# Four graph layers in one pipeline: layer 0 turned by DMA, hi and lo halves in one transfer, two biases moved to GpSimd

## The chip, the cores and the metric

The kernel runs on one core of a Trainium2 chip. The metric is the device time of one execution in microseconds; lower is better. Engines: TensorE (PE in the profile; PEld is its weight load), VectorE (DVE), ScalarE (ACT), GpSimd (POOL), and SyncE (SP), which here only issues DMAs.

## The reference

Input x has 128 graphs of 128 nodes with 256 features, and all graphs share one adjacency matrix. Four layers follow each other, each as x = x + layer(relu(layernorm(x))):

```
L0  h = X W;  e = leaky_relu(att_self + att_neigh^T), masked by adj;  out = [softmax(e) h | h]      W: 256x128
L1  out = deg * (x Wi + b) + adj (x Wj)                                                            W: 256x256 each
L2  8 heads of 32: q, k, v = h W^T + b;  softmax(q k^T / sqrt(32), masked) v;  then Wo, bo
L3  as L0 with one head of 256: softmax(leaky_relu(e_src + e_dst), masked) Wh
```

## The kernel before, in words

The work is cut into 64 groups of two graphs (`GROUP = 2`). A group's activations x stay in SBUF (`x`, 128 partitions x 2 x 256, fp32, 11 buffers), and every other tile of a group is double. All the work of a group is a list of some 110 pieces, such as `stats0_0` or `make_query`, whose last digit before the underscore is the layer.

**Software pipeline.** Each engine has one `slot(at)` function, a list written out by hand: `at(3, make_query)` means that in slot t the engine does this piece for group t - 3. `run(slot)` goes through 64 + 7 slots. So each engine's queue is a fixed order that repeats once a slot, and groups of up to eight ages are in it at a time. An engine's instructions run in the order of its queue; a wait on a semaphore (`wait_ge`) holds back all that stands behind it. A slot number says nothing of time between engines: one engine's slot t can run beside another's slot t + 1.

**Numbers.** Products with big weights are done as fp16 triples (`triple`, lines 402 to 407): each factor is split in a high and a low fp16 half, and hi·hi, hi·lo and lo·hi are added up in PSUM. Weights are scaled by 256 first and unscaled when PSUM is read. To split an activation, ScalarE writes the high half with a ReLU or copy (`rows_hi2`, `keep_out`, `rows_hi3`), and VectorE writes the rest (`rows_lo2`, `split_out`, `rows_lo3`).

**Turns.** A product needs its left operand with features on the partitions. For layers 2 and 3, the mixed heads (`out`) and the attention probabilities, SyncE issues transposing DMAs, one for the high and one for the low half (lines 344 to 374; of 512 columns, the probabilities of 2048). Layer 0 is different: it is fp32, its normalized rows are turned by four TensorE transposes (`turn`, line 400), ScalarE copies them out of PSUM (`relu_hi0`), and `feat0` (line 466) is an fp32 matmul, which the profile records as two instructions.

**Layer norm.** VectorE takes bn_stats and bn_aggr; GpSimd adds eps (`add_eps`), negates the mean (`negate_mean`), takes the power -1/2 (`power`) and normalizes the two graphs (`norm_0`, `norm_1`). GpSimd also adds layer 0's second half to x (`add_feat0`) and makes the low halves of the probabilities (`split_head_0` to `_3`).

**Biases.** Those of layer 1 (degree times b1) and of the output projection are added in PSUM by one matmul of 512 columns each (lines 506 and 607).

**SyncE's order**, which holds every DMA of the loop: move_lo3, move_hi3, load_x, move_out_hi, move_out_lo, move_hi2, move_lo2, store_x, move_heads_hi, move_heads_lo. PSUM has eight banks of 512 fp32 columns, and each piece has a fixed one; where two pieces share a bank, an explicit wait keeps them apart.

Of the kernel before, what the change touches and what calls it, by code (L numbers as in the profile page):

```python
# [5 lines left out]
F32 = mybir.dt.float32  # L6
F16 = mybir.dt.float16
# [33 lines left out]
def build(nc, x_in, adj, adj_t, w0, w0_t, a0, w_i, w_j, b1, w_q, w_k, b_qk, w_v, b_v, w_o, b_o, w3, w3_t, a3, out):  # L41
# [7 lines left out]
    with ctx:  # L49
# [18 lines left out]
        w0_f = sb("w0_f", [P, KC, F0W], F32)  # L68
        w_f = sb("w_f", [P, KC, COLS], F32)
# [9 lines left out]
        bo_row = sb("bo_row", [P, D], F32)  # L79
        out_bias = sb("out_bias", [P, D], F32)  # L80

        unit_rows = sb("unit_rows", [P, KC * GROUP * P], F16)
        deg_rows = sb("deg_rows", [P, P], F16)
        b1_rows = sb("b1_rows", [P, D], F16)
        out_rows = sb("out_rows", [P, D], F16)
        qk_bias = sb("qk_bias", [P, 2 * KC * P], F16)
        qk_bias_f = sb("qk_bias_f", [P, 2 * KC * P], F32)
        ones_h = sb("ones_h", [P, P], F16)
# [5 lines left out]
        nmean0, vareps0, rstd0 = (pair(n, [P, GROUP], F32) for n in ("nmean0", "vareps0", "rstd0"))  # L94
# [3 lines left out]
        nmean1, vareps1, rstd1 = (pair(n, [P, GROUP], F32) for n in ("nmean1", "vareps1", "rstd1"))  # L98
# [3 lines left out]
        nmean2, vareps2, rstd2 = (pair(n, [P, GROUP], F32) for n in ("nmean2", "vareps2", "rstd2"))  # L102
# [3 lines left out]
        nmean3, vareps3, rstd3 = (pair(n, [P, GROUP], F32) for n in ("nmean3", "vareps3", "rstd3"))  # L106
        xn3 = pair("xn3", [P, GROUP, D], F32)

        h0t = pair("h0t", [P, KC * GROUP * P], F32)
# [14 lines left out]
        h2_rows_hi = pair("h2_rows_hi", [P, GROUP, D], F16)  # L124
        h2_rows_lo = pair("h2_rows_lo", [P, GROUP, D], F16)
        h2_hi = pair("h2_hi", [P, GROUP * KC, P], F16)
        h2_lo = pair("h2_lo", [P, GROUP * KC, P], F16)
# [1181 lines left out]
```

## Time and profile before

| | |
|---|---|
| median of 3 runs | 1322.18 us (1316.64 to 1323.46) |
| profiled execution | 1312.74 us |
| its span, first to last instruction | 1310.9 us |
| mean granted TensorE clock | 0.972 |
| busy: TensorE, VectorE, ScalarE, GpSimd | 88%, 80%, 76%, 71% of the span |
| DMA queue of the loop | 61.6% of 16 engines |

Busy time is the union of an engine's instructions. Instructions of one engine overlap in its pipeline, so the distance from one start to the next tells what an instruction costs, and its duration tells when its result is there. In the chain of waits "SPq" is SyncE's queue issuing a DMA, and "issue" is time for which the profile shows no reason.

### The profile page before, as it was taken

What the parts mean: (1) busy time and instruction counts of PE and PEld (TensorE: products, weight loads), DVE (VectorE), ACT (ScalarE), POOL (GpSimd) and SP (SyncE); (2) the same over time, 40 slices, a digit from 0 to 9 for tenths busy, and PEclk for the clock granted to TensorE, in tenths of its full rate; (3) what the DMA queues carried; (4) which work ended last, traced back from release to release, by engine and by line L of the source; (5) the groups of instructions that cost most, each with busy time, mean ns of one, the idle gap of its engine ahead of it and who ended that gap; (6) DMA issues with size and microseconds to landing.
All of it is one profiled execution on the core that took longest, in us unless ns stands there. A gap on an engine that the chain in (4) does not pass through costs nothing.

```text
span 1310.9 us, 39708 instructions
## 1 busy us (share of the span) xinstructions
PE 1158.1 (88%) x15385; PEld 967.8 (74%) x15385; DVE 1052.9 (80%) x2913; ACT 1001.4 (76%) x2824; POOL 936.7 (71%) x1606
## 2 busy tenths in 40 slices
PE   3578999999998999999999999998999998999855
PEld 3467878777877877787777877777878787777743
DVE  3468888888887988898888888888888888888752
ACT  2367888888878878887887888778888887888752
POOL 1357777877776777777778777877787777778540
PEclk7699999999999999999999999999999999999996
DMA  5025766665776666677656766666677556776652
GB/s 178 9 50 106 122 106 123 130 132 117 129 132 115 123 130 131 123 126 131 134 116 128 133 124 124 130 130 121 124 130 138 122 123 128 127 123 122 126 111 51
DMA packets 514492, 156.56 MB, mean 119 GB/s; under 512 B 478208, under 2 KB 514304, under 8 KB 514304
## 3 DMA queue, kind: packets, MB, share of 16 engines
q1 hardware_dynamic: 514304, 154.03, 61.6%
q8 instruction: 122, 2.00, 0.6%
q14 instruction: 66, 0.54, 0.2%
HBM read 19.73 MB, written 16.78 MB: 28 GB/s over the span
## 4 chain that ended last, share of the span: by engine, by line
PE 25%; ACT 19%; DVE 17%; DMA 16%; SPq 16%; POOL 5%; issue 3%; POOLq 0%; DVEq 0%
DMA h_lo<-h_rows_lo 9%; PE ps L405 5%; PE ps L407 5%; PE ps L406 5%; SPq L362 5%; DMA h_hi<-h_rows_hi 5%; SPq L346 5%; SPq L366 4%; ACT head_prob L1066 4%; ACT head_prob L1058 4%; ACT head_prob L1074 4%; DVE h_rows_lo L912 3%; DVE key_lo L850 2%; DVE head_nmax L865 2%; ACT out_rows_hi L1089 2%
## 5 line engine op out<-in xcount | busy, mean ns | idle before, releaser
L405 PE MATMUL ps<-w_hi,h_hi 128*128 128x256 f16 (+1 forms) x512 | 142.3, 278 | 35.2 <-DMA h_hi<-h_rows_hi 34.9
L406 PE MATMUL ps<-w_lo,h_hi 128*128 128x256 f16 (+1 forms) x512 | 141.6, 277 | 0.0
L407 PE MATMUL ps<-w_hi,h_lo 128*128 128x256 f16 (+1 forms) x512 | 141.5, 276 | 0.0
L406 PE MATMUL ps<-h_lo,w_hi 128*128 128x256 f16 x512 | 140.5, 274 | 0.0
L407 PE MATMUL ps<-h_hi,w_lo 128*128 128x256 f16 x512 | 140.5, 274 | 0.0
L405 PE MATMUL ps<-h_hi,w_hi 128*128 128x256 f16 x512 | 140.5, 274 | 0.0
L405 PE MATMUL ps<-w_hi,agg_hi 128*128 128x256 f16 x512 | 139.8, 273 | 0.0
L406 PE MATMUL ps<-w_lo,agg_hi 128*128 128x256 f16 x512 | 139.3, 272 | 0.0
L407 PE MATMUL ps<-w_hi,agg_lo 128*128 128x256 f16 x512 | 139.1, 272 | 0.0
L1223 POOL TENSOR_TENSOR head_lo<-head_prob,head_hi 128x512 f16<-128x512 f32 x64 | 74.1, 1157 | 85.1 <-ACT head_hi L1085 85.1
L1183 POOL TENSOR_TENSOR x<-x,g 128x256 f32<-128x256 f32 x64 | 44.5, 695 | 110.0 <-ACT g L992 110.0
L1085 ACT ACTIVATE head_hi<-head_prob 128x2048 f16<-128x2048 f32 x64 | 122.7, 1918 | 0.0
L854 DVE SCALAR_TENSOR_TENSOR v_lo<-ps,v_hi 128x512 f16<-128x512 f32 x64 | 44.4, 694 | 81.3 <-ACT v_hi L1053 81.3
L405 PEld LDWEIGHTS ps<-w_hi,h_hi 128*128 128x128 f16 x512 | 50.2, 98 | 62.5 <-DMA h_hi<-h_rows_hi 54.6
L405 PE MATMUL ps<-v_hi,head_t_hi 128*128 128x33 f16 x1024 | 84.0, 178 | 1.8 <-DMA head_t_lo<-head_lo 1.7
L407 PE MATMUL ps<-v_hi,head_t_lo 128*128 128x33 f16 x1024 | 84.0, 177 | 0.0
L406 PE MATMUL ps<-v_lo,head_t_hi 128*128 128x33 f16 x1024 | 84.0, 177 | 0.0
L1045 ACT ACTIVATE query_hi<-ps 128x512 f16<-128x512 f32 x64 | 38.2, 597 | 58.9 <-PE ps L407 58.9
L405 PEld LDWEIGHTS ps<-v_hi,head_t_hi 128*128 128x128 f16 x1024 | 79.8, 96 | 3.9 <-issue 3.1
L1049 ACT ACTIVATE key_hi<-ps 128x512 f16<-128x512 f32 x64 | 38.2, 597 | 57.4 <-PE ps L407 57.4
L1074 ACT ACTIVATE head_prob<-ps,head_nmax 128x128 f32<-128x128 f32 x256 | 73.0, 368 | 10.0 <-DVE head_nmax L865 8.7
L1093 ACT ACTIVATE h_rows_hi<-xn 128x512 f16<-128x512 f32 x64 | 40.3, 629 | 52.2 <-POOL xn L1250 51.6
(192 smaller groups left out, 5037.7 us busy)
## 6 DMA issues: line engine op xcount, KB each, us to landing
x<-in_x SPq DMA_DIRECT2D x64, 256.0 KB, 3.0
out<-x SPq DMA_DIRECT2D x64, 256.0 KB, 2.6
h_hi<-h_rows_hi SPq DMA_TRANSPOSE x128, 2.5
h_lo<-h_rows_lo SPq DMA_TRANSPOSE x128, 2.5
head_t_hi<-head_hi SPq DMA_TRANSPOSE x64, 5.6
head_t_lo<-head_lo SPq DMA_TRANSPOSE x64, 4.4
out_hi<-out_rows_hi SPq DMA_TRANSPOSE x64, 2.5
out_lo<-out_rows_lo SPq DMA_TRANSPOSE x64, 2.5
```

The costliest lines, as they stand in the source:

```text
L346: sp.dma_start(h2_hi[g % 2][:, :, :], h2_rows_hi[g % 2][:, :, :].rearrange("p b d -> p (b d)"), transpose=True).then_inc(move_hi2_done[g % ...
L362: sp.dma_start(out_hi[g % 2][:, :, :], out_rows_hi[g % 2][:, :, :].rearrange("p b d -> p (b d)"), transpose=True).then_inc(move_out_hi_don ...
L366: sp.dma_start(out_lo[g % 2][:, :, :], out_rows_lo[g % 2][:, :, :].rearrange("p b d -> p (b d)"), transpose=True).then_inc(move_out_lo_don ...
L405: pe.matmul(o, lh, rh, start=start, stop=False)
L406: pe.matmul(o, lh, rl, start=False, stop=False)
L407: return pe.matmul(o, ll, rh, start=False, stop=stop)
L1058: last = act.activation(head_prob[:, 0, j * P:(j + 1) * P], sc0_ps[:, j * P:(j + 1) * P], ACT.Exp, bias=head_nmax[g % 2][:, 0, j:j + 1])
L1066: last = act.activation(head_prob[:, 1, j * P:(j + 1) * P], sc1_ps[:, j * P:(j + 1) * P], ACT.Exp, bias=head_nmax[g % 2][:, 1, j:j + 1])
L1074: last = act.activation(head_prob[:, 2, j * P:(j + 1) * P], sc2_ps[:, j * P:(j + 1) * P], ACT.Exp, bias=head_nmax[g % 2][:, 2, j:j + 1])
L1085: act.activation(head_hi[:, :, :], head_prob[:, :, :], ACT.Copy).then_inc(cast_heads_done, 1)
L1183: pool.tensor_tensor(x[g % XBUF][:, :, F0:D], x[g % XBUF][:, :, F0:D], g0[g % 2][:, :, 0:F0], ALU.add).then_inc(add_feat0_done, 1)
L1223: pool.tensor_tensor(head_lo[:, 0, :], head_prob[:, 0, :], head_hi[:, 0, :], ALU.subtract)
```

## The change

- **Halves together.** The high and the low half of an activation lie in one tile (`h2_rows`, `mix_rows`, `h3_rows`: 128 x 2 x 2 x 256 fp16) and one DMA of 1024 columns turns both (`move2`, `move_out`, `move3`). The probabilities keep their two DMAs.
- **Layer 0** goes the way of the other layers: `rows_hi0` (ScalarE), `rows_lo0` (VectorE), `move0` (SyncE, 1024 columns), and `feat0` as an fp16 triple with split weights `w0_hi`, `w0_lo`. The TensorE transposes are gone.
- **Biases.** Degree times b1 and the output bias are laid out as fp32 rows (`deg_b1`, `out_bias`) and GpSimd adds them to x (`add_deg_bias`, `add_out_bias`); the two bias matmuls are gone.
- **Layer norm.** Nothing is negated: the mean is subtracted in the normalizing instruction. Adding eps moves from GpSimd to VectorE.
- **Orders.** All five lists are new, with other slot numbers (layer 2's heads and layer 3 one slot later, on TensorE layers 0 and 1 one slot earlier), the PSUM banks are dealt anew, and with them the waits that guard them.

```diff
+            def move0(g):
+                sp.wait_ge(rows_lo0_done, g + 1)
+                sp.dma_start(h0_t[g % 2][:, :, :], h0_rows[g % 2][:, :, :, :].rearrange("p h b d -> p (h b d)"), transpose=True).then_inc(move0_done[g % 2], 16)
...
             def feat0(g):
-                pe.wait_ge(relu_hi0_done, g + 1)
-                if g >= 2:
-                    pe.wait_ge(update1_0_done, g - 1)
+                pe.wait_ge(move0_done[g % 2], 16 * (g // 2) + 16)
+                if g >= 4:
+                    pe.wait_ge(head_exp_3_done, g - 3)
                 for b in range(GROUP):
                     for c in range(KC):
-                        last = pe.matmul(f0_ps[:, b * F0W:(b + 1) * F0W], h0t[g % 2][:, (c * GROUP + b) * P:(c * GROUP + b + 1) * P], w0_f[:, c, :],
-                                         start=(c == 0), stop=(c == KC - 1))
+                        last = triple(f0_ps[:, b * F0W:(b + 1) * F0W], h0_t[g % 2][:, b * KC + c, :], h0_t[g % 2][:, (GROUP + b) * KC + c, :], w0_hi[:, c, :], w0_lo[:, c, :],
+                                      start=(c == 0), stop=(c == KC - 1))
...
             def message_0(g):
-                pe.matmul(m1_ps[:, :].rearrange("p (b n) -> p b n", b=GROUP), deg_rows[:, :], b1_rows[:, :].unsqueeze(1).to_broadcast([P, GROUP, D]),
-                          start=True, stop=False)
+                if g >= 5:
+                    pe.wait_ge(leaky3_0_done, g - 4)
...
             def make_key(g):
-                if g >= 1:
-                    pe.wait_ge(split_value_done, g)
+                if g < graph_groups - 2:
+                    pe.wait_ge(update0_1_done, g + 3)
...
             def head_scores(g):
                 pe.wait_ge(split_key_done, g + 1)
-                if g < graph_groups - 2:
-                    pe.wait_ge(update0_0_done, g + 3)
+                if g < graph_groups - 3:
+                    pe.wait_ge(leaky0_0_done, g + 4)
...
             def project_0(g):
+                pe.wait_ge(move_out_done[g % 2], 16 * (g // 2) + 16)
+                if g < graph_groups - 4:
+                    pe.wait_ge(split_agg_0_done, g + 5)
...
+            def add_eps0(g):
+                dve.wait_ge(mean_var0_done, g + 1)
+                dve.tensor_scalar(vareps0[g % 2][:, :], moments0[g % 2][:, :, 1], EPS, None, ALU.add).then_inc(add_eps0_done, 1)
+
+            def rows_lo0(g):
+                dve.wait_ge(rows_hi0_done, g + 1)
+                dve.scalar_tensor_tensor(h0_rows[g % 2][:, 1, :, :], xn0[g % 2][:, :, :], 0.0, h0_rows[g % 2][:, 0, :, :], ALU.max, ALU.subtract).then_inc(rows_lo0_done, 1)
...
+            def add_deg_bias(g):
+                pool.tensor_tensor(x[g % XBUF][:, :, :], x[g % XBUF][:, :, :], deg_b1[:, :].unsqueeze(1).to_broadcast([P, GROUP, D]), ALU.add).then_inc(add_deg_bias_done, 1)
```

The new lists, piece and slot number:

```
SyncE    load_x 0, move3 7, move_out 6, move_heads_hi 5, move2 3, move_heads_lo 5, move0 0, store_x 7
TensorE  head_sum_0/1 5, make_key 3, feat0 0, make_value 3, logit_rows0 0, aggregate_0 1, feat3_1/0 6, head_scores 3,
         logit_rows3 6, aggregate_1 1, turn_probs0_0/1 0, project_0/1 5, message_0 1, turn_probs3_0/1 6, gat_sum0 0,
         message_1 1, gat_sum3 6, make_query 2
VectorE  update1_1/0 3, rows_lo3 7, stats2_1 3, invert_heads_0 6, stats2_0 3, invert_heads_1 6, head_norm_0 6, mean_var2 3,
         head_norm_1 6, add_eps2 3, relu_lo1 2, split_query 4, split_out 6, stats0_1/0 0, split_key 4, mean_var0 0,
         split_value 4, add_eps0 0, row_max0 1, rows_lo2 3, split_agg_0 2, head_max_1/0 4, row_max3 7, head_max_2 4,
         inv_sum0 1, update2_0 6, split_agg_1 2, update2_1 6, stats3_0/1 6, rows_lo0 0, inv_sum3 7, mean_var3 6,
         update0_0 1, add_eps3 6, head_max_3 4, update0_1 1, stats1_0/1 1, update3_1 7, mean_var1 1, update3_0 7, add_eps1 1
ScalarE  cast_key 4, keep_feat0 1, keep_value 4, leaky0_1/0 1, rows_hi2 3, keep_agg_0 2, keep_feat3_1/0 7, expo0_0/1 1,
         leaky3_1/0 7, keep_agg_1 2, keep_probs0 1, head_exp_1 4, expo3_0/1 7, rows_hi0 0, head_exp_0 4, keep_probs3 7,
         head_exp_2/3 4, rows_hi3 6, cast_heads 4, relu_hi1 1, cast_query 3, keep_out 5
GpSimd   norm1_0 2, add_out_bias 6, power2 3, split_head_1 5, norm2_1/0 3, split_head_0/2 5, power0 0, split_head_3 5,
         norm0_0/1 0, add_feat0 1, add_deg_bias 2, power3 6, norm3_1/0 6, power1 1, norm1_1 1
```

## Rows read from the trace of the kernel before

**Rows 1.** The page: span; busy us, share and count of each engine.

```profile
span 1310.9 us, 39708 instructions
...
PE 1158.1 (88%) x15385; PEld 967.8 (74%) x15385; DVE 1052.9 (80%) x2913; ACT 1001.4 (76%) x2824; POOL 936.7 (71%) x1606
```

**Rows 2.** Window 600 to 800 us: busy us and count, clock, DMA share.

```profile
600.00:800.00 200.00, 186.15 (x2540) 157.57 (x2527) 171.96 (x477) 165.70 (x470) 154.16 (x264) 1.00 0.65 125
```

**Rows 3.** L755, layer 0 statistics: all 64, then the second (start, us).

```profile
L755 DVE BATCH_NORM_STATS2 stats<-x x64: 394/417/426, 19.2 to 1194.4; 128x6 f32<-128x256 f32 x64
...
20.18 0.39 DVE L755 BATCH_NORM_STATS2 stats<-x 128x6 f32<-128x256 f32 x1
```

**Rows 4.** Chain of waits, 630 to 651 us: start, length, what.

```profile
631.60 0.27 PE ps L532
...
638.93 0.62 ACT head_prob L1074 x2
...
642.13 0.52 ACT h_hi L1024
...
643.68 1.20 SPq L362
...
647.53 2.55 DMA h_lo<-h_rows_lo
...
650.22 0.27 PE ps L532
```

**Rows 5.** TensorE's timeline: start, us, line, out<-in, shape, count.

```profile
602.91 0.63 PE L400 MATMUL ps<-ident,xn 128*128 128x128 f32 x4
603.38 1.03 PE L657 MATMUL ps<-g,prob_t 128*128 128x256 f32 x4
...
607.45 1.06 PE L466 MATMUL ps<-w_f,h0t 128*128 128x130 f32 x8
608.34 0.27 PE L405 MATMUL ps<-w_hi,h_hi 128*128 128x256 f16 x1
608.45 0.27 PE L406 MATMUL ps<-w_lo,h_hi 128*128 128x256 f16 x1
```

**Rows 6.** Timeline of GpSimd, then VectorE, 605 to 616 us.

```profile
605.66 1.06 POOL L1219 TENSOR_SCALAR xn<-x,nmean,rstd 128x256 f32<-128x256 f32 x1
...
606.38 0.88 DVE L806 SCALAR_TENSOR_TENSOR h_lo<-xn,h_hi 128x512 f16<-128x512 f32 x1
607.41 0.69 DVE L842 SCALAR_TENSOR_TENSOR h_rows_lo<-xn,h_rows_hi 128x512 f16<-128x512 f32 x1 [0.16 <-ACT h_rows_hi L1041]
608.02 0.48 DVE L929 SCALAR_TENSOR_TENSOR x<-ps,inv,x 128x256 f32<-128x256 f32 x1
...
614.57 0.14 DVE L772 RECIPROCAL inv<-sum 128x2 f32<-128x2 f32 x1
614.63 0.67 DVE L812 TENSOR_TENSOR agg_lo<-ps,agg_hi 128x512 f16<-128x512 f32 x1
```

**Rows 7.** GpSimd's groups: count, busy us, mean ns, idle before.

```profile
L1226 POOL TENSOR_TENSOR head_lo<-head_prob,head_hi 128x512 f16<-128x512 f32 x64 | 74.2, 1159 | 0.0
...
L1176 POOL TENSOR_SCALAR xn<-x,nmean,rstd 128x256 f32<-128x256 f32 x64 | 55.6, 869 | 7.0
L1183 POOL TENSOR_TENSOR x<-x,g 128x256 f32<-128x256 f32 x64 | 44.5, 695 | 110.0 <-ACT g L992 110.0
...
L1216 POOL TENSOR_SCALAR xn<-x,nmean,rstd 128x256 f32<-128x256 f32 x64 | 35.4, 553 | 6.7
...
L1165 POOL TENSOR_SCALAR vareps<-moments 128x2 f32<-128x2 f32 x64 | 12.2, 191 | 23.5 <-DVE moments L760 19.5
```

**Rows 8.** DMA issues (last: us to landing); one issue of SyncE.

```profile
h_hi<-h_rows_hi SPq DMA_TRANSPOSE x128, 2.5
...
head_t_lo<-head_lo SPq DMA_TRANSPOSE x64, 4.4
...
634.03 1.90 SPq L358 DMA_TRANSPOSE head_t_lo<-head_lo  x1
```

More of the change, by code:

```diff
@@ L377, in store_x @@
                 sp.dma_start(out_groups[g], x[g % XBUF][:, :, :]).then_inc(x_moved[g % XBUF], 16)
             def slot(at):
-                at(6, move_lo3)
-                at(6, move_hi3)
                 at(0, load_x)
-                at(5, move_out_hi)
-                at(5, move_out_lo)
-                at(3, move_hi2)
-                at(3, move_lo2)
+                at(7, move3)
+                at(6, move_out)
+                at(5, move_heads_hi)
+                at(3, move2)
+                at(5, move_heads_lo)
@@ L387, in slot @@
+                at(0, move0)
                 at(7, store_x)
[L388 to L389 removed]
             run(slot)
@@ L511, in message_0 @@
                         triple(m1_ps[:, 0 * D:1 * D], agg_hi[g % 2][:, 0, at], agg_lo[g % 2][:, 0, at], w_hi[:, c, col:col + D], w_lo[:, c, col:col + D],
-                                      start=False, stop=False)
+                                      start=(part == 0 and c == 0), stop=(part == 1 and c == KC - 1))
             def message_1(g):
@@ L932, in slot @@
             def slot(at):
+                at(3, update1_1)
+                at(3, update1_0)
+                at(7, rows_lo3)
+                at(3, stats2_1)
+                at(6, invert_heads_0)
+                at(3, stats2_0)
+                at(6, invert_heads_1)
+                at(6, head_norm_0)
+                at(3, mean_var2)
+                at(6, head_norm_1)
+                at(3, add_eps2)
+                at(2, relu_lo1)
+                at(4, split_query)
+                at(6, split_out)
@@ new lines, in slot @@
+                at(0, stats0_1)
+                at(0, stats0_0)
+                at(4, split_key)
+                at(0, mean_var0)
+                at(4, split_value)
+                at(0, add_eps0)
+                at(1, row_max0)
+                at(3, rows_lo2)
+                at(2, split_agg_0)
+                at(4, head_max_1)
+                at(4, head_max_0)
+                at(7, row_max3)
+                at(4, head_max_2)
+                at(1, inv_sum0)
+                at(6, update2_0)
@@ L933, in slot @@
+                at(2, split_agg_1)
+                at(6, update2_1)
                 at(6, stats3_0)
                 at(6, stats3_1)
[L935 to L936 removed]
+                at(0, rows_lo0)
+                at(7, inv_sum3)
                 at(6, mean_var3)
[L938 to L943 removed]
@@ L959, in slot @@
-                at(5, head_norm_1)
-                at(4, head_max_3)
-                at(7, update3_0)
-                at(5, split_out)
-                at(2, relu_lo1)
-                at(3, rows_lo2)
-                at(7, update3_1)
-                at(0, stats0_1)
-                at(0, stats0_0)
-                at(0, mean_var0)
-                at(4, split_value)
-                at(1, row_max0)
-                at(5, update2_1)
-                at(5, update2_0)
-                at(6, row_max3)
+                at(1, update0_0)
@@ L975, in _ @@
+                at(6, add_eps3)
+                at(4, head_max_3)
+                at(1, update0_1)
+                at(1, stats1_0)
+                at(1, stats1_1)
+                at(7, update3_1)
+                at(1, mean_var1)
+                at(7, update3_0)
+                at(1, add_eps1)
             run(slot)
```

532 lines of the change are left out of this document (242 added, 290 removed).

## The prediction

> **What bounds the kernel now.** I began with the page. Over the span of 1310.9 us TensorE is busy 88%, VectorE 80%, ScalarE 76%, GpSimd 71% [rows 1], so no engine is saturated by itself. Then the windows: in an undisturbed 200 us stretch TensorE is busy 186.15, VectorE 171.96, ScalarE 165.70 and GpSimd 154.16 us, the granted clock is 1.00 (the 2.4 GHz level), the DMA engines are busy 0.65 [rows 2]. The kernel is a software pipeline with one slot for each of 64 groups of graphs, so the number to know is the slot. The first statistics line runs 64 times, the second time at 20.18 us and the last at 1194.4 us [rows 3]: 62 slots in 1174.2 us, 18.94 us each. One slot thus holds 186.15/200 x 18.94 = 17.6 us of TensorE, 16.3 of VectorE, 15.7 of ScalarE, 14.6 of GpSimd. 1.3 us of the slot belong to nobody.
>
> Who sets 18.94 stands in the chain of waits. In the stretch shown it closes on itself: from make_query at 631.60 us, through the layer-0 sum and VectorE's queue to ScalarE's exponentials at 638.93, its ReLU at 642.13 and its two next copies, to SyncE, which issues move_out_hi at 643.68, then move_out_lo and move_hi2, and then move_lo2 at 647.53, whose landing lets the next make_query go at 650.22 [rows 4]. That is 18.62 us for one slot. It is a loop made by the order of the queues: the data of move_hi2 was ready long before, but SyncE stood behind move_out. 2.55 us of it are a DMA's flight, 3.8 us are three issues on SyncE. The average slot is 0.3 us above this loop's 18.62, from slots that are disturbed otherwise. So the kernel is bound by a loop through all queues, about 1 us above TensorE's own 17.6.
>
> **The change part by part.**
>
> *TensorE.* Four fp32 turns of layer 0 go: they start at 602.91 and the next work at 603.38 [rows 5], 0.47 us. feat0 was eight fp32 records from 607.45 to 608.34, 0.89 us; it becomes 12 fp16 matmuls of 130 columns. The trace has no such form. The nearest row is fp16 with 256 columns, whose starts lie 0.11 us apart [rows 5]; by columns 130 are 0.056, and the upper bound is the 0.11 of twice the columns. So 0.67 to 1.3 us; no row excludes less, and I let the lower end be half, 0.34. I take 0.67: the cost by columns is the nearest. -0.22. The two bias matmuls (512 columns each, twice a 256-column one) go: -0.44. Sum -1.1 us: TensorE 17.6 to 16.5 us in a slot (bounds 16.2 to 17.2).
>
> *VectorE.* It gains rows_lo0, a 128x512 fused subtract like that of line 842, whose successor starts 0.61 us after it [rows 6], and four add_eps on 128x2. The nearest row is the reciprocal on 128x2, 0.06 us to the next start; the nearest dear one is 0.19, what GpSimd takes for the same operation [rows 6, 7]. So 0.61 + 4 x 0.07 = 0.9 us (0.85 to 1.4): 16.3 to 17.2 us. VectorE becomes the fullest engine.
>
> *ScalarE.* The ReLU that emptied the turned bank becomes a ReLU of the same 128x512 from SBUF; about 0.5 us on the chain before [rows 4], no change: 15.7.
>
> *GpSimd.* Four eps and four negations go, about 0.19 us each [rows 7]: -1.5. Two additions of 128x512 come. The nearest row is the subtraction of the same shape, 1.16 us; from the 128x256 addition, 0.70 [rows 7], the bounds are 0.7 and 1.4. I take 1.16: +2.3 (1.4 to 2.8). GpSimd: 15.4 us. The mean goes in as a subtract in the same instruction, at no price. The biases only have to be in x before update1_1 and update2_0; each add stands most of a slot ahead of them. Should it be late, VectorE waits with its whole slot behind it.
>
> *The shared reads of SBUF.* norm2_1 at 605.66 takes 1.06 us where its twin norm2_0 takes 0.55, and norm0_0 takes 0.87 on the mean; norm2_1 lies across relu_lo1 (606.38) on VectorE, which itself takes 0.88 us where the like of it, rows_lo2, takes 0.69 [rows 6, 7]. Both VectorE lines read two SBUF tensors. rows_lo0 is one more of this kind, and the GpSimd additions are long ones to meet. I price that at one more meeting, 0.5 us on GpSimd, inside its margin, and keep the full price for a rival. The Trainium skill ("GPSIMD Engine Reference", section "Key points") says that GpSimd shares its SBUF interfaces with VectorE and contends with instructions that have two SBUF inputs; by that rule the trace agrees, and it speaks against both the added low half and the added additions.
>
> *SyncE and DMA.* Six 512-column transposes (1.2 us of issue on the chain [rows 4], 2.5 us to landing [rows 8]) and two of 2048 columns (1.90 us and more to issue, 4.4 us and more to landing [rows 8]) become four of 1024 and the same two. No row has 1024. Linear between the two, the issue is 1.2 + 0.7/3 = 1.45 us and the landing 3.1 us; bounds 1.2 and 1.9, 2.5 and 4.4. I take the linear values. SyncE's transposes: 6 x 1.2 + 2 x 1.9 = 11.0 us before, 4 x 1.45 + 3.8 = 9.6 after, well below a slot. The transposed columns grow from 6 x 512 + 4096 = 7168 to 8192, 14%; were all DMA time theirs, its share would go from 0.65 to 0.65 x 1.14 x 18.94/17.6 = 0.80, still not a bound.
>
> *The orders.* The new orders decide whether the 17.2 us can be reached. I laid VectorE's new list out without a gap (0.6 us for a 512-element instruction, 0.33 for a 256-element one) at a slot of 17.5 us and followed each result out and back. TensorE's slot then begins 0.6 us after VectorE's. Old loop: rows_lo2 ends at 8.0 us, move2 lands by 11.2, make_query stands last on TensorE at 15.0: margin 3.8, where it was zero. split_out ends at 5.0, move_out lands at 8.1, project_0 stands at 9.4: margin 1.3. rows_lo3 ends at 1.35, lands at 4.5, feat3_1 at 6.1: margin 1.6. Layer norm 3: add_eps3 ends at 14.1, a power on GpSimd, taken at the 0.7 of its 128x256 addition, and two norms of 0.55 [rows 7], the ReLU 0.6, hops 0.3, against rows_lo3 at 18.2: margin 1.4, part of it eaten by ScalarE's own queue. The low head halves are split by about 10.5, land by 15 and are needed at 18.1: margin 3.1. If a 1024-column transpose took the full 4.4 us, the 1.3 us of project_0 would just be used up. Added waits: make_key on update0_1, head_scores on leaky0_0, project_0 on split_agg_0, head_sum on two exponentials of the next group; each releases at least 0.5 us ahead of its place in this layout, else all of TensorE's slot behind it slips. New bank holders and the split of wait between the halves (head 1 before head 0, and so on) cost nothing by themselves.
>
> So a slot of 17.2 us by VectorE, plus the 0.3 to 0.4 us by which the average lay above the loop: 17.6.
>
> *Ends of the pipeline.* From first statistics to store a group now spans 7.7 slots by the positions in the lists instead of 7.0; at the new slot 135 us instead of 132: +3 us of drain over the 116.5 us between the last statistics and the end [rows 1, 3]. Slot 0 now also holds rows_lo0, which waits for GpSimd and ScalarE: +4 us. Splitting the first weight is 1 us more of setup, covered by weight loads or not.
>
> *Sum.* 20.2 + 4 + 62 x 17.6 + 116.5 + 3 = 1235 us of span. The profiled execution took 1312.74 us, 1.8 more than its span, and the median of the three runs, 1322.18, is 0.72% above it. So 1237 x 1.0072 = **1246 us**, 5.8% less.
>
> **The rivals.**
>
> *A. GpSimd takes over (slower).* It is an in-order queue and now waits for VectorE at power2, power3 and power1. With the additions at 1.4 us it holds 15.9 us; five two-input VectorE instructions in a slot each stretch a GpSimd one by 0.5 us, of which the trace has two (norm2_1 and norm0_0 [rows 6, 7]); three more are 1.5 us; three waits for VectorE's small results, about 0.6 each, 1.8. That makes 19.2 us: 62 x 0.26 + 7 = +23 us, 1346 us. It decides once GpSimd's slot passes 18.9. For it: the doubled norm2_1. Against it: in the trace GpSimd has 4.3 us of a slot free, and its additions are not late for anyone.
>
> *B. The loop through SyncE comes back (no change).* A 1024-column transpose behind a head transpose lands at 4.4 us or later, project_0 or feat3_1 waits in every slot as make_query did, and the slot stays near 18.8: 62 x -0.14 + 7 = -2 us, 1320 us. For it: SyncE's order puts move_heads_hi between move_out and move2. Against: the margins above.
>
> *C. Half of it.* The slot settles at 18.1 to 18.4 because several margins under 1.5 us are eaten by turns: 62 x -0.7 + 7 = -36 us, about 1285 us. For it: the kernel before lay 1.3 us above its fullest engine, and here the same would give 18.5.
>
> *D. Better.* The 0.3 us of disturbance goes too and VectorE meets less contention: 17.2 us, 1220 us.
>
> **How the numbers follow.** Forecast 0.55 (1225 to 1268 us), C 0.2, B 0.1, A 0.1, D 0.05. The forecast, C and D are faster by more than 0.5%, which is about what a measurement of this kernel can tell from no change; of B's 0.1, 0.07 lie within it, 0.01 below and 0.02 above. Faster 0.81, same 0.07, slower 0.12. The range leaves out D's lower end and A: 1220 to 1320 us.
>
> **What would show it.** The first statistics line 62 times at 17.6 us; VectorE busiest, at 95% or more in a mid stretch, TensorE about 93%; make_query waiting for no DMA; waits of project_0 and feat3_1 for a DMA near zero; starts of the 130-column matmuls 0.055 us apart; add_deg_bias and add_out_bias at 1.2 us; 1024-column transposes landing at about 3.1 us. I am wrong if GpSimd is busy over 17 us of a slot or VectorE waits for its additions (A), if TensorE's largest wait is again a DMA (B), or if no engine is above 93% (C).

## The result: 19.6% slower, and the profile after

The changed kernel takes 1579.11 us (median of four runs, 1577.5 to 1581.48), against 1321.39 us (1316.64 to 1323.46) for the kernel before beside it: ratio 1.1958, 95% interval 1.1921 to 1.1994. The forecast was 1246 us, in a range of 1220 to 1320. It had the wrong sign, and the time is far outside the range.

The page of the changed kernel, whose profiled execution took 1581.48 us. Its rows answer to [rows 1]; the line with percentages is the chain of waits by engine over the span.

```profile
span 1579.7 us, 39680 instructions
...
PE 1192.6 (75%) x15256; PEld 966.9 (61%) x15256; DVE 1186.1 (75%) x3229; ACT 1005.6 (64%) x2825; POOL 1401.7 (89%) x1222
...
PEclk9899999998998999999999899989999999998987
...
POOL 73%; issue 10%; DVE 6%; PE 4%; ACT 4%; DMA 1%; SPq 1%; POOLq 0%; DVEq 0%
```

GpSimd issues 1222 instructions instead of 1606, and they keep it busy for 1401.7 us instead of 936.7. Fewer and longer: the cost is in what one of them takes. The window 600 to 800 us and the layer-0 statistics (line 734 here, line 755 before), which answer to [rows 2, 3]:

```profile
600.00:800.00 200.00, 154.17 (x2043) 127.00 (x2041) 156.52 (x427) 133.79 (x384) 187.89 (x164) 0.94 0.57 114
```

```profile
L734 DVE BATCH_NORM_STATS2 stats<-x x64: 411/414/421, 20.8 to 1438.6; 128x6 f32<-128x256 f32 x64
...
26.75 0.42 DVE L734 BATCH_NORM_STATS2 stats<-x 128x6 f32<-128x256 f32 x1
```

The slot is (1438.6 - 26.75)/62 = 22.77 us instead of 18.94. The whole difference of the spans, 268.8 us, is then 62 longer slots, (1438.6 - 26.75) - (1194.4 - 20.18) = 237.6 us, 1.6 us more before the first statistics, 5.0 in slot 0 (5.95 us long, 0.98 before) and 24.6 us of drain (141.1 instead of 116.5). These 62 slots are not all alike: the first five are short (13.9 to 19.6 us, while the pipeline fills) and the others all last 23.2 to 23.3 us, so the window holds slots of 23.3 us and GpSimd is busy 187.89/200 x 23.3 = 21.9 us of one (1401.7/64 gives the same); the forecast gave it 15.4. That is also the sign set down beforehand for rival A, GpSimd busy over 17 us of a slot. TensorE is busy 154.17 of 200 us, and its granted clock of 0.94 mixes the 2.4 GHz level with stretches at the lower one; it is off the path here.

GpSimd's groups by shape, which answer to [rows 7] (mean ns before the last bar):

```profile
L1204 POOL TENSOR_SCALAR xn<-x,moments,rstd 128x256 f32<-128x256 f32 x64 | 106.7, 1667 | 6.7
L1234 POOL TENSOR_TENSOR head_lo<-head_prob,head_hi 128x512 f16<-128x512 f32 x64 | 105.5, 1649 | 2.6 <-ACT head_hi L1102 2.6
...
L1209 POOL TENSOR_TENSOR x<-x,deg_b 128x512 f32<-128x512 f32 x64 | 80.7, 1261 | 0.0
L1216 POOL TENSOR_SCALAR xn<-x,moments,rstd 128x256 f32<-128x256 f32 x64 | 78.0, 1219 | 0.0
L1213 POOL TENSOR_TENSOR rstd<-vareps,minus_half 128x2 f32<-128x2 f32 x64 | 72.3, 1130 | 2.3 <-DVE vareps L832 2.3
L1244 POOL TENSOR_TENSOR rstd<-vareps,minus_half 128x2 f32<-128x2 f32 x64 | 45.7, 714 | 95.9 <-DVE vareps L911 95.9
```

The normalization of one half of a group, 0.553 us before, takes 1.219 us, with the same shape and type; line 1204 takes 1.667. The bias addition takes 1.261 us, near the 1.16 I chose and inside its bounds.

The chain of waits between 820 and 831 us (start, length, what), to be held against [rows 4]:

```profile
820.72 1.61 issue
...
822.78 0.16 DVE vareps L911
...
823.01 0.72 POOL rstd L1244
...
823.83 1.23 POOL xn L1251
825.06 1.20 POOL xn L1247
...
827.05 1.70 POOL xn L1204
```

The loop through SyncE is gone. A loop on GpSimd stands in its place: the power of layer norm 3 starts at 799.72 and at 823.01 us, and nearly all between is GpSimd's own work. What is not is the "issue" of 1.61 us, which the timelines of GpSimd and VectorE explain:

```profile
820.59 1.26 POOL L1209 TENSOR_TENSOR x<-x,deg_b 128x512 f32<-128x512 f32 x1
823.01 0.71 POOL L1244 TENSOR_TENSOR rstd<-vareps,minus_half 128x2 f32<-128x2 f32 x1 [1.16 <-DVE vareps L911]
```

```profile
820.68 1.72 DVE L747 SCALAR_TENSOR_TENSOR h_rows<-xn,h_rows 128x512 f16<-128x512 f32 x1 [1.23 <-ACT h_rows L997]
...
822.78 0.15 DVE L911 TENSOR_SCALAR vareps<-moments 128x2 f32<-128x2 f32 x1
```

rows_lo0 (line 747) starts beside GpSimd's add_deg_bias and takes 1.72 us, where the like of it takes 0.69 [rows 6]; add_eps3 (line 911) stands behind it, and GpSimd waits 1.16 us for that. rows_lo0 had itself waited 1.23 us for ScalarE's ReLU of what GpSimd had just normalized, so its place ahead of add_eps3 counts beside its length. So there are two suspects: the new form of the normalization, and the meetings of GpSimd's additions with VectorE, with the orders that bring them about.

### The profile page after: what moved, and what is told of

Same layout as the page of the kernel before. It is cut to its first block, busy times and chain, and to the rows that moved or that the text cites. A ratio compares the mean times of both kernels' runs of the same rounds, so it can differ in the third digit from the quotient of the medians.

```text
span 1579.7 us, 39680 instructions
## 1 busy us (share of the span) xinstructions
PE 1192.6 (75%) x15256; PEld 966.9 (61%) x15256; DVE 1186.1 (75%) x3229; ACT 1005.6 (64%) x2825; POOL 1401.7 (89%) x1222
## 4 chain that ended last, share of the span: by engine, by line
POOL 73%; issue 10%; DVE 6%; PE 4%; ACT 4%; DMA 1%; SPq 1%; POOLq 0%; DVEq 0%
POOL xn L1204 7%; POOL head_lo L1234 6%; POOL xn L1220 5%; POOL head_lo L1237 5%; POOL xn L1216 5%; POOL xn L1247 5%; POOL x L1225 5%; POOL xn L1251 5%; POOL rstd L1213 4%; POOL xn L1186 4%; POOL xn L1189 4%; POOL head_lo L1228 4%; POOL head_lo L1240 4%; POOL rstd L1244 3%; POOL rstd L1197 3%
## 5 line engine op out<-in xcount | busy, mean ns | idle before, releaser
L398 PE MATMUL ps<-w_hi,h_t 128*128 128x256 f16 (+2 forms) x768 | 208.0, 287 | 42.7 <-DMA h_t<-h_rows 42.7
L399 PE MATMUL ps<-w_lo,h_t 128*128 128x256 f16 (+2 forms) x768 | 210.5, 285 | 0.0
L400 PE MATMUL ps<-w_hi,h_t 128*128 128x256 f16 (+2 forms) x768 | 210.1, 285 | 0.0
L747 DVE SCALAR_TENSOR_TENSOR h_rows<-xn,h_rows 128x512 f16<-128x512 f32 x64 | 106.8, 1669 | 67.3 <-ACT h_rows L997 67.3
L838 DVE SCALAR_TENSOR_TENSOR h_rows<-xn,h_rows 128x512 f16<-128x512 f32 x64 | 62.3, 974 | 110.8 <-ACT h_rows L1052 110.8
L1052 ACT ACTIVATE h_rows<-xn 128x512 f16<-128x512 f32 x64 | 40.3, 630 | 165.1 <-POOL xn L1216 165.1
L400 PE MATMUL ps<-h_t,w_lo 128*128 128x256 f16 x512 | 139.5, 273 | 0.0
L399 PE MATMUL ps<-h_t,w_hi 128*128 128x256 f16 x512 | 139.4, 272 | 0.0
L398 PE MATMUL ps<-h_t,w_hi 128*128 128x256 f16 x512 | 139.3, 272 | 0.0
L797 DVE SCALAR_TENSOR_TENSOR h_lo<-xn,h_hi 128x512 f16<-128x512 f32 x64 | 68.8, 1074 | 90.8 <-ACT h_hi L1035 90.8
L1244 POOL TENSOR_TENSOR rstd<-vareps,minus_half 128x2 f32<-128x2 f32 x64 | 45.7, 714 | 95.9 <-DVE vareps L911 95.9
L398 PEld LDWEIGHTS ps<-w_hi,h_t 128*128 128x128 f16 x768 | 83.1, 108 | 59.7 <-DMA h_t<-h_rows 33.3
L639 PE MATMUL ps<-g,prob_t 128*128 128x256 f32 x256 | 72.7, 407 | 61.1 <-ACT prob_t L1138 61.1
L1204 POOL TENSOR_SCALAR xn<-x,moments,rstd 128x256 f32<-128x256 f32 x64 | 106.7, 1667 | 6.7
L1110 ACT ACTIVATE h_rows<-xn 128x512 f16<-128x512 f32 x64 | 40.3, 630 | 106.7 <-POOL xn L1247 106.7
```

The source lines that it names most:

```text
L398: pe.matmul(o, lh, rh, start=start, stop=False)
L399: pe.matmul(o, lh, rl, start=False, stop=False)
L400: return pe.matmul(o, ll, rh, start=False, stop=stop)
L747: dve.scalar_tensor_tensor(h0_rows[g % 2][:, 1, :, :], xn0[g % 2][:, :, :], 0.0, h0_rows[g % 2][:, 0, :, :], ALU.max, ALU.subtract).then_i ...
L1204: pool.tensor_scalar(xn1[g % 2][:, 1, :], x[g % XBUF][:, 1, :], moments1[g % 2][:, 1, 0:1], rstd1[g % 2][:, 1:2], ALU.subtract, ALU.mult)
L1244: pool.tensor_tensor(rstd3[g % 2][:, :], vareps3[g % 2][:, :], minus_half[:, :], ALU.pow).then_inc(power3_done, 1)
```

## The experiments

All ratios are against the kernel before, on the same chip. Experiments 1 to 4 and 12, 5 to 8, and 9 to 11 ran on three different chips, where the kernel before took 1318.17 (1318.05 beside experiment 12), 1320.81 and 1321.01 us, so times of different chips can be compared to about 0.3%. Experiments 2, 3, 7, 8 and 10 were measured once and have no interval; the others were measured four times. "Slot" is the distance from the second to the last layer-0 statistics, over 62. In the window of 600 to 800 us a slot is longer than this mean, since the first ones are short: 23.3 us after the change, 18.57 in experiment 1, 18.12 in 5, 18.71 in 6 and 17.32 in 8 (starts of the same line). Shares of the window are turned into us of a slot with these.

**1. The negated mean back, on VectorE.** The changed kernel, with four small negations on VectorE, and the eight normalizations adding a negated mean.

```diff
+                dve.tensor_scalar(nmean0[g % 2][:, :], moments0[g % 2][:, :, 0], -1.0, None, ALU.mult)
...
-                ... x[g % XBUF][:, 0, :], moments0[g % 2][:, 0, 0:1], rstd0[g % 2][:, 0:1], ALU.subtract, ALU.mult)
+                ... x[g % XBUF][:, 0, :], nmean0[g % 2][:, 0:1], rstd0[g % 2][:, 0:1], ALU.add, ALU.mult)
```

> The changed kernel with one thing undone: the mean is negated again (four small VectorE instructions on 128x2) and the eight normalizing instructions add the negated mean instead of subtracting the mean. Theory (the subtracting form of the GpSimd instruction costs 1.22 us where the adding form cost 0.55): the eight norms fall back to about 0.55 us, GpSimd's slot loses about 5.2 of 23.3 us, and the time falls to 1270 to 1340 us. Rival 1 (the norms are slow because of contention with VectorE and the new orders): they stay at 1.2 us and the time stays at 1560 to 1580 us. Rival 2 (the two bias additions and their place are what costs): the norms fall but the time stays above 1450 us.

Measured: 1278.05 us, ratio 0.9699 (0.9655 to 0.9744), slot 18.22. This one undone edit turns 19.6% slower into 3.0% faster: 4.55 us of slot. A normalization without a meeting is back at 0.56 us, and VectorE takes over as the bound, 197.09 of 200 us:

```profile
L1251 POOL TENSOR_SCALAR xn<-x,nmean,rstd 128x256 f32<-128x256 f32 x64 | 35.7, 558 | 0.0
```

```profile
600.00:800.00 200.00, 179.76 (x2539) 152.30 (x2535) 197.09 (x583) 168.57 (x479) 174.93 (x206) 1.00 0.75 145
```

**2. The same negations on GpSimd**, where they stood before.

```diff
-                dve.tensor_scalar(nmean0[g % 2][:, :], moments0[g % 2][:, :, 0], -1.0, None, ALU.mult)
+                pool.tensor_scalar(nmean0[g % 2][:, :], moments0[g % 2][:, :, 0], -1.0, 0.0, ALU.mult, ALU.add)
```

> As the run before, but the four negations stand on GpSimd, each ahead of the power of its layer, as in the kernel before the change. Theory: 4 x 0.19 us more on GpSimd than with the negation on VectorE, about 0.8 us a slot or 50 us in all if GpSimd bounds the slot; nothing if another engine does. Rivals as for the run before.

Measured once: 1276.71 us, slot 18.21, against 1278.05 and 18.22. Where the negations stand makes no difference that shows.

**3. Is it the operation or the operand?** Each layer of the changed kernel gets another form. Layer 1 adds a mean that is not negated, so its result is not the reference's.

```diff
 # layer 0: subtract, the mean copied to a tile of its own
+... nmean0[g % 2][:, 0:1], rstd0[g % 2][:, 0:1], ALU.subtract, ALU.mult)
 # layer 1: add, read from the moments
+... moments1[g % 2][:, 0, 0:1], rstd1[g % 2][:, 0:1], ALU.add, ALU.mult)
 # layer 2: add, a negated mean in a tile of its own
+... nmean2[g % 2][:, 0:1], rstd2[g % 2][:, 0:1], ALU.add, ALU.mult)
 # layer 3: as changed, subtract, from the moments
```

> The changed kernel with four forms of the norm in one program, to see which part of the form costs. Layer 0: subtract, with the mean copied to a tile of its own. Layer 1: add, with the operand read from the moments tile (the mean is not negated, so this part of the result is not the reference's). Layer 2: add, with the negated mean in a tile of its own. Layer 3: subtract from the moments tile, as changed. Theory (the subtract operation is the slow one): layers 0 and 3 at 1.2 us, layers 1 and 2 at 0.55. Rival (the operand's place with its stride is slow): layers 1 and 3 at 1.2, layers 0 and 2 at 0.55. Time between the changed kernel and the run with all four undone, near 1420 us.

Measured once: 1412.17 us, slot 20.25. One line of each form, in the order of the layers 0, 3, 2, 1:

```profile
L1188 POOL TENSOR_SCALAR xn<-x,nmean,rstd 128x256 f32<-128x256 f32 x64 | 79.2, 1237 | 0.5
...
L1249 POOL TENSOR_SCALAR xn<-x,moments,rstd 128x256 f32<-128x256 f32 x64 | 78.0, 1219 | 0.0
...
L1222 POOL TENSOR_SCALAR xn<-x,nmean,rstd 128x256 f32<-128x256 f32 x64 | 35.8, 559 | 0.2
L1202 POOL TENSOR_SCALAR xn<-x,moments,rstd 128x256 f32<-128x256 f32 x64 | 35.2, 550 | 0.0
```

A subtract takes 1.22 to 1.24 us with either operand, an add 0.55 to 0.56 with either. It is the operation. (The first half of layer 1, which also adds, takes 0.995 us here. It is the one that is long in every version with these orders, 0.789 us in experiment 1; the last section shows what it meets.) Half of the normalizations in the slow form cost 20.25 - 18.22 = 2.03 us of slot, while they add 4 x 0.67 = 2.7 us to GpSimd: so about 0.65 us of it presumably goes into idle time of GpSimd, which had 25 of 200 us in experiment 1.

**4. The new form alone, in the kernel before.** The negations stay where they were, and nothing reads them.

```diff
-... nmean0[g % 2][:, 0:1], rstd0[g % 2][:, 0:1], ALU.add, ALU.mult)
+... moments0[g % 2][:, 0, 0:1], rstd0[g % 2][:, 0:1], ALU.subtract, ALU.mult)
```

> The kernel before, with this one part of the change alone: the eight norms subtract the mean from the moments tile; the negations are still made and not read. Theory: GpSimd goes from 14.6 to about 19.8 us of a slot and bounds it; with its waits the slot is 20.5 to 21.5 us, the time 1420 to 1480 us. Rival 1 (slow only in the new orders): the norms stay at 0.55 us and the time at 1322 us.

Measured: 1604.87 us, ratio 1.2179 (1.2114 to 1.2244), slot 23.45. The direction was right and the size far short: I had summed GpSimd's work and forgotten that its slot would be a serial one.

```profile
L1216 POOL TENSOR_SCALAR xn<-x,moments,rstd 128x256 f32<-128x256 f32 x64 | 78.7, 1229 | 6.7
```

```profile
600.00:800.00 200.00, 157.63 (x2027) 127.90 (x2029) 136.28 (x385) 132.24 (x373) 167.01 (x211) 0.98 0.56 104
```

GpSimd is busy only 167.01 of 200 us here and still sets the slot, together with the ScalarE work that stands between its normalizations and its splits:

```profile
717.23 1.57 POOL xn L1219
...
718.83 0.63 ACT h_rows_hi L1041
719.46 0.28 ACT g L1097
...
720.28 1.81 ACT head_hi L1085
...
722.16 1.16 POOL head_lo L1223
```

From 718.80 to 722.16 us GpSimd does nothing but add_feat0, 0.69 us at 720.36: the ReLU waits for the last normalization, head_hi stands behind that ReLU in ScalarE's queue, and the split waits for head_hi. So the added 5.3 us came on top of a round trip. GpSimd is idle 33 of 200 us here and 46 before the change, 3.9 and 4.3 us of a slot, so hardly any of its idle time was used up.

**5. rows_lo0 out of add_deg_bias's way.** Experiment 1, with VectorE's order changed in one place.

```diff
                 at(6, stats3_1)
-                at(0, rows_lo0)
                 at(7, inv_sum3)
                 at(6, mean_var3)
                 at(1, update0_0)
                 at(6, add_eps3)
+                at(0, rows_lo0)
```

> The kernel with the negation back on VectorE (1278 us), and on VectorE rows_lo0 stands six places later, behind add_eps3. There VectorE is busy 98% of the time, and rows_lo0 takes 1.6 us where its like takes 0.69, as it stands beside GpSimd's add_deg_bias. Theory (a VectorE instruction that reads two SBUF tensors waits for a GpSimd instruction that does too, and that meeting is the lost time): rows_lo0 falls to 0.7 to 1.0 us, GpSimd gets its power3 up to 1 us sooner, and the time falls to 1220 to 1260 us. Rival (rows_lo0 is slow by its output or by its own nature, or the slot has another bound): it stays at 1.6 us, the time at 1275 to 1281 us.

Measured: 1252.35 us, ratio 0.9487 (0.9464 to 0.951), slot 17.81, 0.41 us less than in experiment 1. The timelines of experiment 1, GpSimd first, show what the move takes away:

```profile
716.89 1.26 POOL L1213 TENSOR_TENSOR x<-x,deg_b 128x512 f32<-128x512 f32 x1
```

```profile
717.04 1.66 DVE L748 SCALAR_TENSOR_TENSOR h_rows<-xn,h_rows 128x512 f16<-128x512 f32 x1
718.62 0.15 DVE L927 RECIPROCAL inv<-sum 128x2 f32<-128x2 f32 x1
```

rows_lo0 starts while the addition runs (716.89 to 718.15 us), and VectorE's next instruction starts 1.58 us after it instead of 0.61. The mean of the line was 1.595 us in experiment 1; moved it is

```profile
L748 DVE SCALAR_TENSOR_TENSOR h_rows<-xn,h_rows 128x512 f16<-128x512 f32 x64 | 43.8, 685 | 2.8 <-ACT h_rows L1001 2.8
```

A part of the gain goes to new meetings: the negation of layer 3 now takes 0.541 us instead of 0.154 on VectorE, and the power of layer norm 3 on GpSimd 1.039 instead of 0.701.

**6. The other addition moved too.** Experiment 1, with rows_lo0 behind head_max_3 and add_out_bias one slot earlier, beside add_deg_bias.

```diff
-                at(6, add_out_bias)
...
                 at(1, add_feat0)
+                at(5, add_out_bias)
                 at(2, add_deg_bias)
```

> As the run before, with rows_lo0 one place further back, behind head_max_3, and with add_out_bias taken from the head of GpSimd's slot to stand between add_feat0 and add_deg_bias, beside VectorE's statistics and PSUM reads. Theory of the meetings: the negation of layer 2 on VectorE (0.69 us beside add_out_bias) falls to about 0.2, rows_lo0 to 0.7, and the time to 1190 to 1250 us. Rival (GpSimd, now with both additions in a row ahead of power3, delays layer 3's norm): rows_hi3 waits more and the time stays at 1260 us or above.

Measured: 1282.64 us, ratio 0.9728 (0.9695 to 0.9761), slot 18.34. Missed: no faster than experiment 1 and 30 us slower than experiment 5. Its timelines, GpSimd first:

```profile
701.51 1.26 POOL L1229 TENSOR_TENSOR x<-x,out_bias 128x512 f32<-128x512 f32 x1
702.74 1.25 POOL L1213 TENSOR_TENSOR x<-x,deg_b 128x512 f32<-128x512 f32 x1
```

```profile
702.18 0.62 DVE L914 TENSOR_SCALAR nmean<-moments 128x2 f32<-128x2 f32 x1
702.71 1.31 DVE L915 TENSOR_SCALAR vareps<-moments 128x2 f32<-128x2 f32 x1
```

I had kept only the large two-input instructions of VectorE away from the additions. The two on 128x2, with one input, end when the additions end: 0.62 and 1.31 us for what takes 0.15 elsewhere. The meetings were moved, not avoided.

```profile
600.00:800.00 200.00, 180.07 (x2576) 150.88 (x2574) 196.30 (x575) 165.89 (x478) 176.44 (x205) 1.00 0.72 141
```

VectorE is full and busy 196.30/200 x 18.71 = 18.4 us of a slot, against 196.38/200 x 18.12 = 17.8 in experiment 5; that is the whole of the longer slot. The rival of the expectation shows too: the additions end at 703.99 us, so the power could not have started before, and the ReLU of layer 3 waits 29.3 us in all for its normalization instead of 5.4. No run tells the two apart.

**7. Experiment 5 with the negations on GpSimd** (the edit of experiment 2).

```diff
-                dve.tensor_scalar(nmean3[g % 2][:, :], moments3[g % 2][:, :, 0], -1.0, None, ALU.mult)
+                pool.tensor_scalar(nmean3[g % 2][:, :], moments3[g % 2][:, :, 0], -1.0, 0.0, ALU.mult, ALU.add)
```

> The negations on GpSimd and rows_lo0 behind add_eps3. Beside the first run of this set it has 4 x 0.07 us less on VectorE, and 4 x 0.19 more on GpSimd. Theory (VectorE bounds): a few us faster than that run. Rival (GpSimd is close behind): 10 us slower or more.

Measured once: 1251.97 us, slot 17.81, as experiment 5, where I expected a few us less.

**8. Experiment 1 without the bias additions.** This leaves the two biases out of the output.

```diff
-                at(6, add_out_bias)
...
-                at(2, add_deg_bias)
```

> The kernel with the negation back on VectorE and both bias additions of GpSimd left out, and not done elsewhere, so its output lacks the biases of layer 1 and of the output projection. It prices the additions with all that they delay. Theory: rows_lo0 falls to 0.69 us and layer 2's negation to 0.15; VectorE's slot loses 1.4 of 18.5 us, and the time is 1190 to 1220 us. Rival (the additions hide in GpSimd's free time): 1270 us or above.

Measured once: 1200.3 us, slot 17.01, 1.21 less than experiment 1.

```profile
600.00:800.00 200.00, 193.48 (x2741) 163.65 (x2742) 196.94 (x625) 179.46 (x516) 158.33 (x198) 1.00 0.78 153
```

VectorE is busy 196.94/200 x 17.32 = 17.1 us of a slot, against 197.09/200 x 18.57 = 18.3 in experiment 1, with the same instructions on it. rows_lo0 falls from 1.595 to 0.675 us and the negation of layer 2 from 0.691 to 0.176. Two GpSimd instructions cost VectorE 1.2 us a slot, and VectorE is the bound.

**9. The biases in TensorE again.** Experiment 5 without the additions, each bias as one fp16 matmul of 512 columns into the bank that the update reads.

```diff
-                at(6, add_out_bias)
...
+                pe.matmul(pr_ps[:, :].rearrange("p (b n) -> p b n", b=GROUP), unit_rows[:, 0:P], out_rows[:, :].unsqueeze(1).to_broadcast([P, GROUP, D]),
+                          start=True, stop=False)
```

> The best kernel so far (negation on VectorE, rows_lo0 behind add_eps3; 1252 us) with the two biases back in PSUM by one 512-column matmul each, and no addition on GpSimd. Leaving the additions out altogether, with rows_lo0 in its old place, gave 1200 us. Theory (the additions cost VectorE its waits, TensorE has room for 2 x 0.22 us): 1195 to 1220 us. Rival (TensorE, busy 97% of a stretch there, becomes the bound and gives it back): 1230 us or above.

Measured: 1215.12 us, ratio 0.9191 (0.9161 to 0.922), slot 17.19.

```profile
600.00:800.00 200.00, 192.39 (x2762) 162.74 (x2760) 195.35 (x617) 177.27 (x503) 163.90 (x195) 1.00 0.80 154
```

The matmuls are the cheaper place by 37 us, though TensorE is now at 192.39 of 200, next to VectorE's 195.35.

**10. The changed kernel as it is, with rows_lo0 moved** (the edit of experiment 5, the subtract kept).

```diff
-                at(0, rows_lo0)
...
                 at(6, add_eps3)
+                at(0, rows_lo0)
```

> The changed kernel as it is, the subtracting norms included, with rows_lo0 behind add_eps3 on VectorE. GpSimd bounds it, and once a slot GpSimd waits 1.2 to 1.5 us for add_eps3, which stands behind the 1.7 us of rows_lo0. Theory: this wait goes, 1.0 to 1.5 us of 23.3 in a slot, 1485 to 1520 us. Rival (the meeting costs only where VectorE bounds): 1570 us or above.

Measured once: 1533.06 us, slot 22.06: 46 us less where I expected 60 to 95. The waits of GpSimd for add_eps3 fall from 95.9 us in 64 to 26.3 us in 6, but the power behind them, which now stands beside rows_lo0, takes 1.102 us instead of 0.714, 25 us in all; 69.6 less 25 is about the 46 measured. It is the order that helps here and not the end of a meeting: rows_lo0 still takes 1.42 us on the mean (1.67 before it was moved). What is left is GpSimd alone, 197.91 of 200 us:

```profile
600.00:800.00 200.00, 159.64 (x2082) 131.19 (x2080) 159.20 (x444) 138.96 (x395) 197.91 (x169) 0.93 0.58 118
```

**11. The joint transpose taken apart.** Experiment 5, with each of the four 1024-column transposes issued as two of 512.

```diff
-                sp.dma_start(h2_t[g % 2][:, :, :], h2_rows[g % 2][:, :, :, :]..., transpose=True)...
+                sp.dma_start(h2_t[g % 2][:, 0*GROUP*KC:1*GROUP*KC, :], h2_rows[g % 2][:, 0, :, :]..., transpose=True)...
+                sp.dma_start(h2_t[g % 2][:, 1*GROUP*KC:2*GROUP*KC, :], h2_rows[g % 2][:, 1, :, :]..., transpose=True)...
```

> The best kernel so far (1252 us) with each of the four joint transposes issued as two of 512 columns, back to back behind the same wait. SyncE then issues ten transposes a slot. Theory (SyncE has room: about 0.9 us more for each pair, 4 us of a slot of 18): the landings come about 0.5 us later and the time rises by 0 to 25 us. Rival (SyncE's queue becomes the bound as in the kernel before): 1300 us or above.

Measured: 1267.09 us, ratio 0.9589 (0.9555 to 0.9623), slot 17.95. The joint DMA is worth 15 us, in the profiled executions 8.6 us in the slots (62 x 0.138) and 7.4 in the drain (128.5 against 121.1). TensorE's waits for a transposed h (busiest row of each, experiment 11 and then experiment 5; total us, times, longest):

```profile
PE ps L402 <- DMA h_t<-h_rows: 71.8, 63, 11.3
```

```profile
PE ps L398 <- DMA h_t<-h_rows: 37.2, 17, 10.3
```

**12. Experiment 9 with the negations on GpSimd.**

```diff
-                dve.tensor_scalar(nmean0[g % 2][:, :], moments0[g % 2][:, :, 0], -1.0, None, ALU.mult)
+                pool.tensor_scalar(nmean0[g % 2][:, :], moments0[g % 2][:, :, 0], -1.0, 0.0, ALU.mult, ALU.add)
```

> The kernel with the bias matmuls (1215 us) with the four negations on GpSimd, ahead of each power, instead of on VectorE. VectorE, busy 195 of 200 us there, gets four starts of 0.07 us less, some 0.3 us of a slot of 17.2, and GpSimd, busy 164 of 200, four of 0.19 more. Theory (VectorE bounds): 1197 to 1211 us. Rival (GpSimd's results are on the loop too, as power2 waits for add_eps2 and ScalarE waits for norm2_0): the two cancel, 1212 to 1225 us.

Measured: 1205.29 us, ratio 0.9137 (0.9094 to 0.9179), slot 17.07: the fastest complete version, 8.6% below the kernel before. Its interval overlaps that of experiment 9 (0.9161 to 0.922), so the last 10 us are likely rather than certain.

## Why the prediction was wrong

**The step that failed** is in the part on GpSimd: "The mean goes in as a subtract in the same instruction, at no price." It has a price of 1.22 - 0.55 = 0.67 us, eight times a slot: 5.3 us on an engine that I gave 15.4 us. That makes 20.7, and the 21.9 measured is 1.2 above it, most of it the meetings below. With this term the 17.6 us of slot could not have been held. Three runs carry it: the form alone makes the kernel before 21.8% slower (experiment 4), the form undone makes the changed kernel 3.0% faster than before (1), and of operation, tile and stride it is the operation (3). The trace of before had no subtracting TENSOR_SCALAR on GpSimd at all, only ones that add and multiply; by my own rule for what a trace does not show I should have bounded it from both sides, and I put it at zero because it looked like the same instruction. The subtractions that the trace did have, split_head, are of another form, TENSOR_TENSOR, and they misled in the other direction: there a subtract of 512 elements takes 1.16 us [rows 7], no more than the addition's 1.26. Even from those a bound would have come out: 1.16 us for 512 elements is 0.58 for 256 at the low end, and 1.16, were the cost not by elements, at the high end; eight times 0.61 us would have moved GpSimd to 20.3 us and the range with it.

**Rival A** had the right engine and the point from which it decides, a GpSimd slot above 18.9 us. Its mechanism (contention and waits, 19.2 us of slot, 1346 us) was not the one that acted, or only the smaller part of it; at 0.1 it was also given too little.

**The second mis-sized term** is the contention. I priced it as 0.5 us on GpSimd and nothing on VectorE. I had also put norm2_1's 1.06 us in [rows 6] down to relu_lo1 alone; a second VectorE instruction with two SBUF inputs, split_out, runs for 0.73 us at 605.72, right at its start. VectorE pays: 1.2 us a slot for the two additions (8 against 1), 0.41 of it for one place in the order (5 against 1). GpSimd pays too, as the groups after show: line 1204 takes 1.667 us where line 1216 takes 1.219 for the same work, and the power on line 1213 takes 1.130 where that on line 1244 takes 0.714. These two lines stay long without the additions: the first half of layer 1 takes 0.786 us in experiment 8, where its like takes 0.55, and that power 1.043. So it is not the additions that make them long, but what VectorE does beside them. In experiment 1, with the form taken out, VectorE is at 18.3 us of a slot. My 17.2, with four negations at 0.07, would be 17.5, and for the kernel without the additions it would be the same, since I gave them no price on VectorE; measured there is 17.1. So without the additions my layout of VectorE was 0.4 us too dear, which I have not taken apart, and it hides a part of what they cost.

**What held.** The loop through SyncE is gone (rival B is out). TensorE's terms came out: in experiment 5 the 12 matmuls of 130 columns start 0.06 us apart,

```profile
600.10 0.23 PE L398 MATMUL ps<-w_hi,h_t 128*128 128x130 f16 x1 [0.25 <-DMA h_t<-h_rows]
600.17 0.22 PE L399 MATMUL ps<-w_lo,h_t 128*128 128x130 f16 x1
600.22 0.22 PE L400 MATMUL ps<-w_hi,h_t 128*128 128x130 f16 x1
```

and TensorE's busy time there is 184.16/200 x 18.12 = 16.7 us of a slot, for 16.5 forecast. A transpose of 1024 columns takes SyncE 1.23 us and lands in 2.8 to 3.2 us at the changed kernel's slow pace,

```profile
809.67 1.23 SPq L364 DMA_TRANSPOSE mix_t<-mix_rows  x1
```

```profile
h_t<-h_rows SPq DMA_TRANSPOSE x192, 2.8
...
mix_t<-mix_rows SPq DMA_TRANSPOSE x64, 3.2
```

and in 3.5 and 3.2 us at experiment 5's; forecast were 1.45 and 3.1. The new orders do reach a slot under 18 us, but only with rows_lo0 moved: 1252.35 us in experiment 5, 0.5% above the forecast of 1246. That nearness is partly luck: it is a kernel with the negations back, and the dear layout and the unpriced meetings work against each other in it. Slot 0 cost 5.0 us more (forecast 4), the drain 24.6 instead of 3. At the slot of experiment 5 the same reckoning, 7.7 slots for a group instead of 7.0, gives 7.7 x 17.81 - 7.0 x 18.94 = 4.6 us, and its drain is 4.6 us longer (121.1 instead of 116.5). At the changed kernel's slot it gives 7.7 x 22.77 - 132.6 = 43 us, well over the 24.6 measured: it holds near the forecast slot and not when GpSimd sets the slot, and why is open.

**How the 19.6% divide.** From the changed kernel (slot 22.77), undoing the form gives 18.22, the place of rows_lo0 17.81, the biases back in TensorE 17.19. The changed kernel lies 5.17 us above the forecast slot of 17.6: 4.55 of it are the form (22.77 - 18.22), 0.41 the meeting of rows_lo0 with add_deg_bias (18.22 - 17.81), and 0.21 are left. The shares depend on the order in which things are undone: with rows_lo0 moved first, its place is worth 0.71 (22.77 - 22.06) and the form 4.25 (22.06 - 17.81). The part of the change that is a gain is what experiment 12 keeps: the joint transposes, layer 0 turned by DMA with the fp16 products, eps on VectorE, and the orders. Of these only the joint transposes were priced alone (experiment 11). The two parts that cost are the mean without its negation and the biases on GpSimd.

## What to carry to other kernels

An edit that turns an instruction into "the same one with another operation" adds an operation that the trace has never shown: bound it from both sides, and multiply by its count before calling it free. The four negations that the change saved take about a fifth of a us each, and putting them back on GpSimd made no difference that shows (experiment 2), so look first at what the instructions that take over their work will cost. When work is moved to GpSimd because it has idle time, reckon with up to its duration on VectorE too where their instructions can meet (here 1.2 us for two additions of 1.26), and treat their relative place in the two orders as part of the price; a bias that fits in one matmul into a bank already being written was the cheaper place here.

## What the runs showed of the hardware

A TENSOR_SCALAR on GpSimd with subtract and then mult takes 1.22 us on 128x256 fp32, with add and then mult 0.55 (experiment 3, 64 of each line). The Trainium skill ("GPSIMD Engine Reference", section "Elementwise — side-by-side cycle accounting") has the body of such a loop bound by its ports as long as it does no more than two operations on an element, which would give the two forms the same time; the measurement decides otherwise, and why subtract is dearer no run here shows.

Some VectorE instructions that start beside GpSimd's addition end only once it has ended. In experiment 1 the addition ends at 716.89 + 1.26 = 718.15 us and rows_lo0, started at 717.04, ends at 718.70, 0.55 us later. In experiment 6 the two additions end at 702.77 and 703.99 us, and the two 128x2 instructions with one input at 702.80 and 704.02. Others are not held up: a reciprocal, two aggregations of statistics and an update that reads PSUM start under the first of these additions, at 701.66 to 701.94 us, and take 0.14, 0.18, 0.15 and 0.32 us, as elsewhere. It goes the other way too: GpSimd's line 1204 is 0.45 us longer than line 1216, and in the changed kernel a VectorE instruction with two SBUF inputs starts just ahead of it (rows_lo3, VectorE first):

```profile
803.66 0.69 DVE L915 SCALAR_TENSOR_TENSOR h_rows<-xn,h_rows 128x512 f16<-128x512 f32 x1 [0.69 <-ACT h_rows L1110]
```

```profile
803.75 1.70 POOL L1204 TENSOR_SCALAR xn<-x,moments,rstd 128x256 f32<-128x256 f32 x1
```

The Trainium skill ("SBUF — State Buffer", section "Who interferes with whom") says of the ports that VectorE and GpSimd share that whoever comes first keeps them for its whole instruction and the other one blocks, and that a tensor_scalar of VectorE can be among those that take them; the trace agrees with both halves. By that rule the price of a meeting is what is left of the other's instruction, up to 1.26 us here, and not the 0.5 us that I took.

The issue of a DMA transpose on SyncE hardly grew from 512 to 1024 columns: 1.20 us [rows 4] and 1.23.
